# Attention's square layers with half-array tile matmuls, and new instruction lists

## What is computed

```python
# x (32,3,224,224), txt (32,128,192); D = 192
loc  = pw(dw3x3(gelu(patch_conv(x))))                 # 14x14 tokens, 192 channels
g    = gelu(1x1(wavelet_packet(x))); g = gelu(pw(dw3x3(g))); glob = 1x1(g)
h    = (1 - gate) * loc + gate * glob
h    = relu(pw(dw3x3(h))); h = relu(pw(dw3x3(h))); h = pw(dw3x3(loc + h))
tok  = concat([cls, layernorm(h)]); h = concat([tok, txt])       # 325 tokens an image
n    = layernorm(h)
q, k, v = (gelu(n @ w1 + b1) @ w2 + b2 for each of three)        # 192 x 192 layers
y    = (mask * (q @ k.T) / scale) @ v                            # band of 64 tokens
h    = h + layernorm(y)
h    = h + ternary_mlp(layernorm(h))                             # 192 -> 2*512 -> 192
```

## Time and profile before

| | |
|---|---|
| median of 3 runs | 1259.73 us (1259.23 to 1260.78) |
| profiled execution, its own time | 1260.41 us |
| span of its trace, first to last instruction | 1258.5 us |
| TensorE busy | 1139.4 us, 91% of the span |
| VectorE busy | 1007.7 us, 80% |
| ScalarE busy | 1001.6 us, 80% |
| GpSimd busy | 895.9 us, 71% |
| one full turn | 67.6 us |
| granted TensorE clock, mean | 0.945 |

### The profile page before, as it was taken

One profiled execution on the slowest core, in us unless ns is written; L12 is line 12 of the kernel. 1 busy time (PEld: TensorE's weight loads), 2 busy tenths in 40 slices (PEclk: granted clock), 3 DMA queues, 4 the chain that ended last, 5 costly groups with the idle time before them and its releaser, 6 DMA issues.

```text
span 1258.5 us, 19622 instructions
## 1 busy us (share of the span) xinstructions
PE 1139.4 (91%) x5674; PEld 857.1 (68%) x5674; DVE 1007.7 (80%) x2868; ACT 1001.6 (80%) x2581; POOL 895.9 (71%) x924
## 2 busy tenths in 40 slices
PE   3577999999999999999999999999999997979544
PEld 2455787778777878787777778777878785656222
DVE  0666678898989899898989898989999897855643
ACT  2364777898999898989899899989898988776543
POOL 2345477888878787878887888878887877765421
PEclk8797999999999999999999999999999998989655
DMA  8110101010101010101000010101010000000000
GB/s 311 39 44 1 46 1 46 2 56 6 57 6 54 7 52 11 49 14 47 15 26 34 6 57 6 57 6 53 8 49 14 10 15 9 16 8 11 11 8 13
DMA packets 21514, 40.26 MB, mean 32 GB/s; under 512 B 2656, under 2 KB 18208, under 8 KB 19104
## 3 DMA queue, kind: packets, MB, share of 16 engines
q1 hardware_dynamic: 21408, 39.01, 9.0%
HBM read 31.02 MB, written 7.99 MB: 31 GB/s over the span
## 4 chain that ended last, share of the span: by engine, by line
PE 83%; DVE 6%; ACT 5%; issue 2%; DMA 2%; POOL 2%; SPq 1%; DVEq 0%; POOLq 0%; ACTq 0%
PE bank L388 14%; PE bank L490 7%; PE bank L408 7%; PE bank L409 7%; PE bank L366 4%; PE bank L367 4%; PE bank L411 3%; PE bank L413 3%; PE bank L412 3%; PE bank L502 3%; PE bank L511 3%; PE bank L432 2%; PE bank L433 2%; PE bank L369 2%; DVE bank L1219 2%; PE bank L370 2%
## 5 line engine op out<-in xcount | busy, mean ns | idle before, releaser
L1219 DVE SCALAR_TENSOR_TENSOR bank<-padA,c_col,bank 128x406 f32<-128x406 f32 x560 | 358.5, 640 | 9.7
L388 PE MATMUL bank<-x_sb,w_emb 128*128 128x392 f32 x576 | 215.3, 507 | 21.2 <-ACT padB L727 19.9
L803 ACT ACTIVATE prod<-padB,c_col 128x196 f32<-128x196 f32 x432 | 178.1, 458 | 8.9 <-DVE padB L1240 5.1
L1672 POOL TENSOR_TENSOR yg<-y_f,c_gout 128x512 f32<-128x512 f32 (+1 forms) x96 | 122.1, 1272 | 58.8 <-DVE y_f L1409 46.4
L388 PEld LDWEIGHTS bank<-x_sb,w_emb 128*128 128x128 f32 x576 | 105.4, 196 | 77.2 <-ACT padB L727 21.8
L803 ACT ACTIVATE early<-padB,c_col 128x196 f32<-128x196 f32 x288 | 125.1, 459 | 6.1 <-POOL accB L1703 6.0
L490 PE MATMUL bank<-w_in,xq 128*128 128x512 bf16 (+1 forms) x384 | 109.1, 410 | 7.7 <-ACT xq L866 7.7
L1390 DVE SCALAR_TENSOR_TENSOR ya<-th,bank 128x512 f32<-128x512 f32 (+1 forms) x96 | 65.3, 680 | 62.6 <-ACT th L872 62.4
L1209 DVE TENSOR_SCALAR bank<-padA,c_col 128x406 f32<-128x406 f32 x80 | 51.1, 639 | 56.4 <-ACT padA L734 48.8
L872 ACT ACTIVATE th<-bank,sm 128x512 f32<-128x512 f32 (+1 forms) x96 | 66.0, 688 | 25.8 <-PE bank L490 25.5
L502 PEld LDWEIGHTS bank<-c_id,r 128*128 128x128 f32 (+1 forms) x384 | 42.2, 148 | 62.6 <-ACT r L852 46.0
(11 more groups left out here) (226 smaller groups left out, 3535.8 us busy)
## 6 DMA issues: line engine op xcount, KB each, us to landing
x_sb<-xt SPq DMA_DIRECT2D x16, 1176.0 KB, 5.4
out<-o_sb SPq DMA_DIRECT2D x64, 96.0 KB
w_sq<-squares SPq DMA_DIRECT2D x1, 3840.0 KB, 15.7
h_sb<-txt SPq DMA_DIRECT2D x32, 51.8 KB
out<-o_sb SPq DMA_DIRECT2D x32, 51.8 KB
h_sb<-txt SPq DMA_DIRECT2D x32, 44.2 KB
w_in<-win SPq DMA_DIRECT2D x1, 1024.0 KB, 17.7
c_row<-broads SPq DMA_DIRECT2D x1, 672.0 KB, 19.3
```

The lines of the kernel that those rows point to most:

```text
L388: done = mm(pE[:, 0:2 * N_PATCH], w_emb[:, k, m, :], x_sb[:, k, :], start=k == 0, stop=k == KC - 1)
L803: made = go(grid(prod[ACC[s] ^ 1][:, k, :]), tap_view(padB[min(s, 2)], SIDE, k), ACT.Copy, scale=tapcol(s, 1, k))
L1219: v.scalar_tensor_tensor(grid(acc if k == TAPS - 1 else run), tap_view(pad, ROWS_A, k), tapcol(s, 0, k), grid(run), ALU.mult, ALU.add).the ...
L1672: g.tensor_tensor(yg[0:m, :], y_f[0:m, :], c_gout[0:m, :], ALU.mult).then_inc(f_yg, 1)
```

## The change

Three things. First, `mlp` is split in two functions. `mlp_wide` does units 0 and 1 together: both `AA` matmuls, then `B0A` on partitions 0 to 63 alone into the one bank and `B1A` on partitions 64 to 127 alone into the other. They are 64x128 row tiles, which lie in different halves of the array's rows. `mlp_half` does unit 2: `AB0` writes output partitions 0 to 63 alone and `AB1` partitions 64 to 127 alone, as 128x64 column tiles into one bank, and `BB` stays as it was. The number of matmuls is the same, seven a layer. Second, `unit_free` for both banks now stands ahead of the matmuls of `mlp_wide`. Third, all five lists are written anew: the frames of the engines' turns are shifted against each other, the stages are numbered 0 to 6 (22 turns have work, in the first of which PE has only the embedding's BB block), and within a turn BB moves from the turn's start to its second half.

```diff
-DEPTH = 11
+DEPTH = 7
...
+        HALF = (slice(0, DB), slice(DB, P))
...
-            def mlp(a, name, u0, src, c):
+            def mlp_wide(a, name, u0, src):
 
                 w = w_sq[:, SQUARES.index(name)]
-                dst = pT[(u0 + c) % 2][:, 0:T]
-                unit_free(a, u0 + c)
-                if u0 == U_Q1 and c == 0:
-                    took(a, U_XT + 2)
-                if c < 2:
-                    mm(dst, w[:, AA, :], src[:, c, :], start=True, stop=False)
-                    mm(dst, w[:, B0A + c, :], src[:, 2, :], start=False, stop=True).then_inc(at_full, 1)
-                else:
-                    mm(dst, w[:, AB0, :], src[:, 0, :], start=True, stop=False)
-                    mm(dst, w[:, AB1, :], src[:, 1, :], start=False, stop=False)
-                    mm(dst, w[:, BB, :], src[:, 2, :], start=False, stop=True).then_inc(at_full, 1)
+                dst = [pT[(u0 + c) % 2][:, 0:T] for c in range(2)]
+                for c in range(2):
+                    unit_free(a, u0 + c)
+                    if u0 == U_Q1 and c == 0:
+                        took(a, U_XT + 2)
+                    mm(dst[c], w[:, AA, :], src[:, c, :], start=True, stop=False)
+                for c in range(2):
+                    mm(dst[c], w[HALF[c], B0A + c, :], src[HALF[c], 2, :], start=False, stop=True).then_inc(at_full, 1)
+
+            def mlp_half(a, name, u0, src):
+
+                w = w_sq[:, SQUARES.index(name)]
+                dst = pT[(u0 + 2) % 2][:, 0:T]
+                unit_free(a, u0 + 2)
+                for c in range(2):
+                    mm(dst[HALF[c]], w[:, AB0 + c, HALF[c]], src[:, c, :], start=True, stop=False)
+                mm(dst, w[:, BB, :], src[:, 2, :], start=False, stop=True).then_inc(at_full, 1)
...
-                if on[7]:
-                    mlp(it - 7, "kw1", U_K1, xT, 0)
-                if on[9]:
-                    ffn_out(it - 9, 2)
-                if on[7]:
-                    mlp(it - 7, "kw1", U_K1, xT, 1)
+                if on[3]:
+                    mlp_wide(it - 3, "kw1", U_K1, xT)
+                if on[0]:
+                    embed_chunk(it, EMB_BB, range(4, 6))
+                if on[3]:
+                    mlp_half(it - 3, "kw1", U_K1, xT)
```

More of the change, by code:

```diff
@@ L585, in turn @@
-                if on[9]:
-                    rounded_token_transposes(it - 9, 1)
-                if on[5]:
[L588 to L593, removed]
+                if on[5]:
+                    ffn_in(it - 5, 0)
+                if on[4]:
+                    values(it - 4, 1)
+                    values(it - 4, 2)
@@ L602, in turn @@
+                if on[4]:
+                    mixed_values(it - 4, 0)
                 if on[5]:
[L603 to L611, removed]
+                    ffn_out(it - 5, 0)
+                if on[4]:
+                    mixed_values(it - 4, 1)
@@ new lines, in turn @@
+                if on[1]:
+                    if first(it - 1):
+                        weight_totals()
+                if on[5]:
+                    ffn_out(it - 5, 1)
+                    rounded_token_transposes(it - 5, 3)
+                if on[3]:
+                    transposes(it - 3, 0)
+                if on[5]:
+                    ffn_in(it - 5, 3)
+                if on[3]:
+                    transposes(it - 3, 1)
+                if on[1]:
+                    layer_G(it - 1)
@@ new lines, in turn @@
+                if on[3]:
+                    transposes(it - 3, 2)
+                if on[0]:
+                    embed_chunk(it, EMB_BB, range(0, 2))
+                if on[5]:
+                    rounded_hidden_transposes(it - 5, 2)
+                if on[3]:
+                    mlp_wide(it - 3, "qw1", U_Q1, xT)
+                if on[5]:
+                    ffn_out(it - 5, 2)
+                if on[0]:
+                    embed_chunk(it, EMB_BB, range(2, 4))
+                if on[5]:
+                    rounded_token_transposes(it - 5, 4)
@@ new lines, in turn @@
+                if on[3]:
+                    mlp_out(it - 3, U_K1, hk, "kb1", ACT.Gelu, 0)
+                if on[1]:
+                    products(it - 1, L_, range(3, 4))
+                if on[5]:
+                    round_hidden(it - 5, 3)
+                if on[3]:
+                    mlp_out(it - 3, U_K1, hk, "kb1", ACT.Gelu, 1)
+                if on[1]:
+                    products(it - 1, L_, range(4, 5))
+                if on[2]:
+                    products(it - 2, F2_, range(6, 7))
@@ new lines, in turn @@
+                if on[3]:
+                    mlp_out(it - 3, U_K1, hk, "kb1", ACT.Gelu, 2)
+                if on[1]:
+                    glob_out(it - 1)
+                if on[5]:
+                    rounded_hidden(it - 5, 3)
+                if on[2]:
+                    products(it - 2, F2_, range(7, 8))
+                if on[1]:
+                    products(it - 1, L_, range(5, 6))
+                if on[2]:
+                    products(it - 2, F2_, range(8, 9))
+                if on[3]:
+                    mlp_out(it - 3, U_V1, hv, "vb1", ACT.Gelu, 0)
@@ new lines, in turn @@
+                if on[3]:
+                    mlp_out(it - 3, U_V1, hv, "vb1", ACT.Gelu, 2)
+                if on[0]:
+                    embed_out(it, EMB_BB)
+                if on[5]:
+                    gate_tanh(it - 5, 5, odd)
+                if on[3]:
+                    queries_out(it - 3, 0)
+                    queries_out(it - 3, 1)
+                if on[5]:
+                    round_hidden(it - 5, 4)
+                if on[3]:
+                    queries_out(it - 3, 2)
+                if on[2]:
+                    products(it - 2, F3_, range(0, 1))
+                    products(it - 2, F3_, range(1, 2))
```

1124 lines of the change are left out of this document (532 added, 592 removed).

## The result

The changed kernel takes 1251.32 us (median of 4 runs, 1250.83 to 1253.23), the kernel before in the same session 1260.26 us (1259.23 to 1261.88). The ratio is 0.9925 [0.9912, 0.9937]: faster by 0.75%, 9 us. The profiled execution took 1251.12 us, its span is 1249.2 us, and its mean clock 0.949.

A forecast was written before the change was run, and what follows sets the result against it. TensorE was taken as the bound: 67.6 - 2.74 (overlap) + 1.6 (switches), with 0.2 of waits, gives 66.7 us a turn. 0.9 us x 14 turns plus 1 saves 14 us, forecasting 1246 us; range 1210 to 1295, the forecast's own 1229 to 1258.

The forecast's parts named there:

- What bounds the kernel: Full turns: TensorE busy for all 67.61 us, so its microseconds are time in 14 of the 16 turns with attention.
- Part 1, the overlap: Row and column tile couples in five layers: three intervals instead of four, saving 2.74 us a turn (range 0 to 5.5).
- Part 2, the changes of shape: 20 switches a turn between full array and tiles, 0.08 us each for an uncovered load: 1.6 us a turn.
- my first rival: "The drain": each switch waits out the matmul's tail and loads uncovered, +2.4 us a turn, 1294 us; chance 0.17.
- Part 3a, the waits of the new lists: Units 0 and 1 end together, so the second `AA` waits for an eviction, notably in kw2: 0.2 us a turn.
- Part 3b, the load of `x_sb`: Single-buffered load between LA and the next BB: 5.6 us, hidden with under 1 us to spare, costing nothing.
- Part 3c, the ends: Pipeline's first and last turns: one more turn, holding only BB on TensorE at first; 0, within 5 us either way.
- The costs cancel, or the lists decide: Rival: a late load or ends grown by 5 us eat a small gain; 1258 to 1268 us; chance 0.04.
- Full overlap: Rival: tiles don't wait for each other's second instruction; 64.5 us a turn, 1215 us; chance 0.20.
- The drain: Rival: every switch of shape pays tail and uncovered load, 4.9 us a turn; turn 69.9, time 1294 us; chance 0.17.
- the full overlap with the drain: Rival: tile couples overlap fully (-5.5 us a turn) and switches cost +4.9; turn 67.2, time 1254 us; chance 0.10.

The follow-up runs named there:

- experiment 5: Kernel before with the weight sums moved later, plus column tiles alone in unit 2 of the five attention layers, instruction order unchanged: 1236.08 us, ratio 0.9801.
- experiment 3: Changed kernel with its row tiles kept and full-array matmuls in place of the column tiles: 1269.61 us (single run).
- experiment 10: Changed kernel with `mlp_wide` ordered AA, row tile, AA, row tile, so row tiles are not adjacent: 1319.97 us (single run).
- experiment 1: Changed kernel's new lists kept, but every tile turned back into the full-array matmul of before: 1283.96 us, ratio 1.0184.
- experiment 2: Kernel before with its old lists and both kinds of tiles, `mlp_wide` at unit 0's place and `mlp_half` at unit 2's: 1280.46 us, ratio 1.016.
- experiment 6: experiment 5 with row tiles as well in all five layers, both issued by the second unit, each unit at its place: 1267.34 us, ratio 1.0039.
- experiment 7: Changed kernel with `weight_sums` put back at the head of ScalarE's first turn: 1265.78 us, ratio 1.0042.
- experiment 4: Kernel before with only `weight_sums` moved later on ScalarE, behind the first pair's G products: 1247.69 us, ratio 0.9902.
- experiment 9: Changed kernel with two swaps: `ffn_out` ahead of layer F1 on TensorE, first input norm ahead of F1's evictions on ScalarE: 1262.34 us, ratio 1.0008.

## Why the prediction came out as it did

The time was forecast at 1246 and is 1251.3; the direction is right. The steps behind it are mostly not: several errors cancel.

**What bounds the kernel: right.** TensorE is the bound of the full turns, and in experiment 5 what five couples of tiles save there (1.0 us by the starts) comes out as 0.71 us a turn, the rest as idle time of TensorE; 11.6 us of time in 16 pairs. The step from a microsecond of TensorE to a microsecond of time holds only where no wait appears in its place.

**Part 1, the overlap: wrong by a factor of two.** I took three of four intervals, 2.74 us a turn, from instructions in the order A1 A2 B1 B2. The narrow window shows both tiles starting within 7 ns, both for the first and for the second instruction: A1 B1 A2 B2, full overlap, 5.5 us a turn, the upper bound. Experiments 3 and 10 agree with that size. The rule that I cited from the Trainium skill, "TensorE: Matmul & The Clock Gate", Part 3, has tiles start about 4 ns apart; here it is 7 ns. What I concluded from its starts in program order did not hold for the two halves of a float32 matmul. Whether the program or the engine interleaves them, the rows don't tell.

**Part 2, the changes of shape: too cheap by a factor of two.** I took 0.08 us; the starts show about 0.18 (bounds 0 and 0.24), 3.6 instead of 1.6 us a turn. I had only the uncovered load; there are 0.09 to 0.10 us in front of each change as well. That is the mechanism of my first rival, the tail waited out, with two thirds of the tail's recorded 0.16; that it is the tail is read from where the delay stands, no run isolates it. The Trainium skill, "TensorEngine Tiling (Array Packing)", Key Properties, says that a change of mode drains the engine, and these 0.10 us agree; it gives no price.

The two errors nearly cancel: net 1.9 us by the starts and 2.0 by experiment 1, where I had 1.14.

**Part 3a, the waits of the new lists: the step that failed.** I priced them at 0.2 us a turn by looking at the second `AA` and at kw2. They are 2.1 us, and experiment 1 shows that they come with the lists alone. Most lie where I did not look: a token transpose directly behind the `ffn_out` whose eviction it waits for, and the `xh` transposes behind it. The place I did name holds one of 0.34 us in kw2. This eats the whole gain of the tiles, so the turn is 67.65 and not 66.7. Experiments 2 and 6 show that both kinds of tiles could not simply stay in the old lists either: TensorE idles 2.3 and 2.5 us of a turn there.

**Part 3b, the load of `x_sb`: right.** No wait for its DMA appears in the waits of the full turn. The room was larger than my "under 1 us": in the turn from 555.15 the load is issued at 566.91, the median to landing is 5.3 us, and BB's first matmul starts at 575.92, 3.7 us later than that. Of these 1.35 are the two waits above. I did not try a later load.

**Part 3c, the ends: the other step that failed.** I put 0, within 5 us. The fill is 17.2 us shorter and the end 8.2 us longer, together the whole measured gain. Of the fill, 14.5 us are the place of `weight_sums` (experiment 7; 13.9 in experiment 4), a call that stands elsewhere in the new lists and that I did not price: in the trace of before its 12.10 us wait stood on ScalarE, and the rows that I argued from start at 117.70. The end is the lists' too (226.2 in experiment 1, 222.1 in 7, but 213.9 in 4 and 215.3 in 5). From LA to kw2 a pair now takes 177.5 us instead of 166.7, and from kw2 to its last `ffn_out` 145.3 instead of 149.9, so each pair is in the pipeline 6 us longer; that this is the cause of the 8 us is argued from those numbers and not tried.

**The rivals.** "The costs cancel, or the lists decide" (0.04) comes nearest to the turn as it was measured, but with a fill that no case had. "Full overlap" (1215) had the overlap right and neither the switch nor the lists. Nearest in mechanism and in time is the case beside "The drain", the full overlap with the drain (turn 67.2, time 1254, chance 0.10): it had both terms of the tiles (-5.5 and +4.9, where +3.6 was measured), and missed the waits and the ends as my sum did. That 1251.3 lies within the forecast's own range (1229 to 1258) is therefore luck in part: none of its terms for the turn, and not that for the ends, was the measured one. With what was measured, my own sum would have been: -5.5 + 3.6 + 2.1 = +0.2 us for a turn, eleven full turns, +2, and -9 for the ends, which hold the other turns: 1253, within 2 us of the result. What stays open is which chain of evictions sets the turn of the new lists; experiment 9 moved its waits and made it longer.

## What to carry to other kernels

Two half-array matmuls side by side save a whole matmul, but each group of them pays two changes of shape, so tile only where the saved intervals are longer than that (here 0.55 us against 0.36; at 196 columns 0.33 against 0.36, and nothing was left), and keep partners adjacent. Prefer the tiles that lie within one bank and one unit, since they change no one's deadline: column tiles with the order untouched gained 0.7 us a turn, while row tiles in all five layers of the same lists made two banks come full together and cost more in waits than they saved (in lists written for them they gained 0.9). And when a diff moves a one-time piece of work, read the first 40 us of the trace before pricing the turns: a wait for a DMA ahead of the first eviction cost 13 us, more than the 9 us that the whole change won.

## What was not expected of the hardware

- The two instructions of two float32 tile matmuls run pairwise, 7 ns apart, for row tiles and for column tiles, so that the overlap is complete.
- A change between full array and tiles costs about 0.18 us: the next instruction starts 0.09 to 0.10 us late, its weight load isn't hidden, and where both are float32 the instruction behind it is late by another 0.05 to 0.10 us.
- Loads of tiles are shorter, by the median of their records (source view of the changed kernel, ns least/median/longest):

```profile
L412 PEld LDWEIGHTS bank<-xT,w_sq x192: 182/186/335, 113.8 to 1130.2; 64*128 64x128 f32 x192
...
L420 PEld LDWEIGHTS bank<-xT,w_sq x192: 132/135/138, 116.1 to 1132.3; 128*64 128x64 f32 x192
```

A load of half the rows is hardly shorter than a full one (186 ns, where the page's group of the embedding's 128x128 loads has a mean of 191), and one of half the columns takes 135: of these shapes the load's time goes by its columns and not by its rows, though not in proportion. That fits the smaller excess behind the column tiles' change, 0.05 against 0.10 us.
